# A quantised feed-forward layer spread over VectorE, GpSimd and ScalarE, and partly prepared inside the attention layer ahead of it

## The reference, cut to what matters

```
x = x + _L2_xattn_ref(_layernorm(x), ctx, ctx, mask, w_q, w_k, w_v, w_o, b_o)   # 32 heads, 8 wide
x = x + _L2_ffn_ref(_layernorm(x), w_gate, w_up, w_down)

def _act_quant(x):
    scale = 127.0 / clip(max(abs(x), axis=-1), EPS)
    return round(clip(x * scale, -128, 127)) / scale
def _bitlinear(x, w):
    return einsum('bsi,oi->bso', _act_quant(_rmsnorm(x)), _weight_quant(w))
gate = silu(_bitlinear(x, w_gate))      # 256 -> 1024
up   = _bitlinear(x, w_up)              # 256 -> 1024
return _bitlinear(gate * up, w_down)    # 1024 -> 256
```

## Time and profile before

| what | value |
|---|---|
| three runs | 1563.2, 1559.81, 1560.84 us; median 1560.84 us |
| the profiled execution | 1566.56 us, its span 1564.2 us |
| mean granted TensorE clock | 0.953 of full |
| PE busy / weight loads / DVE / ACT / POOL | 1392.5 / 878.8 / 995.0 / 728.9 / 434.4 us |
| first piece of the chain that ended last | PE 58%, DVE 23%, ACT 7%, POOL 6% |

### The profile page before, as it was taken

The page is one execution under the profiler, slowest core; times in us unless marked ns, Lnnn a source line. Parts: engine busy times, 40 slices in busy tenths (PEclk is TensorE's granted clock), DMA queues, the critical chain, the costliest instruction groups (busy, mean ns, idle before and its releaser), DMA issues.

```text
span 1564.2 us, 25737 instructions
## 1 busy us (share of the span) xinstructions
PE 1392.5 (89%) x9822; PEld 878.8 (56%) x9840; DVE 995.0 (64%) x1782; ACT 728.9 (47%) x1746; POOL 434.4 (28%) x385
## 2 busy tenths in 40 slices
PE   7869999999899789999999998988975888988889
PEld 3534555655566446665656864745652645546636
DVE  6784322225678777777776787937778676685542
ACT  3452111112777455655664456358756453362230
POOL 3230000100000387777770000100290045324100
PEclk9979999999999999999999999999997797988989
DMA  7020221003000300000001000020010100000000
GB/s 251 24 85 1 68 59 31 1 0 160 3 2 2 122 7 7 8 7 8 8 1 44 32 22 0 1 81 2 2 53 18 55 1 2 3 1 3 29 0 27
DMA packets 21852, 48.10 MB, mean 31 GB/s; under 512 B 1506, under 2 KB 16995, under 8 KB 20580
## 3 DMA queue, kind: packets, MB, share of 16 engines
q1 hardware_dynamic: 21732, 46.47, 8.5%
HBM read 41.22 MB, written 5.24 MB: 30 GB/s over the span
## 4 chain that ended last, share of the span: by engine, by line
PE 58%; DVE 23%; ACT 7%; POOL 6%; issue 5%; DMA 0%; DVEq 0%; ACTq 0%; POOLq 0%
PE PS L788 42%; DVE work L2349 5%; PE PS L1006 5%; PE PS L871 3%; PE PS L1311 2%; PE PS L800 2%; ACT work L1588 2%; DVE small L1900 2%; PE PS L1065 1%; POOL work L667 1%; POOL WB L661 1%; POOL work L664 1%; POOL WB L660 1%; PE PS L1340 1%; DVE WA L2252 1%
## 5 line engine op out<-in xcount | busy, mean ns | idle before, releaser
L788 PE MATMUL PS<-XT,WB 128*128 128x512 f32 (+1 forms) x688 | 298.3, 591 | 4.8 <-DVE XT L1926 2.4
L788 PEld LDWEIGHTS PS<-XT,WB 128*128 128x128 f32 (+1 forms) x688 | 126.1, 189 | 147.8 <-issue 143.9
L1588 ACT ACTIVATE work<-PS,small 128x128 f32<-128x128 f32 x512 | 138.0, 419 | 45.5 <-DVE small L2149 45.5
L2119 DVE TENSOR_TENSOR work<-PS,work 128x512 f32<-128x512 f32 x48 | 33.1, 692 | 168.0 <-PE PS L788 168.0
L611 POOL TENSOR_SCALAR small<-small 128x4 f32<-128x4 f32 x22 | 5.1, 231 | 413.8 <-DVE small L1903 413.7
L1544 ACT ACTIVATE work<-PS 128x512 f32<-128x512 f32 x48 | 28.7, 597 | 193.6 <-PE PS L788 193.6
L2149 DVE TENSOR_REDUCE small<-PS 128x4 f32<-128x512 f32 x128 | 80.5, 685 | 40.6 <-PE PS L788 40.5
L788 PE MATMUL PS<-XT,WA 128*128 128x512 f32 (+2 forms) x224 | 97.9, 599 | 4.8 <-DVEq L2352 2.5
L2349 DVE SCALAR_TENSOR_TENSOR work<-PS,vec,work 128x508 f32<-128x508 f32 (+2 forms) x108 | 80.2, 743 | 14.0 <-DVE work L2349 6.8
L1006 PE MATMUL PS<-WB,work 128*128 128x256 f32 x384 | 86.9, 379 | 0.5 <-DVE work L2124 0.5
L788 PE MATMUL PS<-WA,XT 128*128 128x256 f32 (+1 forms) x384 | 81.4, 374 | 3.9 <-DVE XT L2169 3.0
(11 more groups left out here) (364 smaller groups left out, 2938.9 us busy)
## 6 DMA issues: line engine op xcount, KB each, us to landing
WB<-in_l0f SPq DMA_DIRECT2D x8, 768.0 KB, 7.5
WB<-in_l1x SPq DMA_DIRECT2D x1, 6144.0 KB, 18.1
WB<-in_l0f SPq DMA_DIRECT2D x32, 96.0 KB, 6.6
WB<-in_l2f SPq DMA_DIRECT2D x1, 3072.0 KB, 10.1
WA<-in_l3a SPq DMA_DIRECT2D x1, 2624.0 KB, 9.0
WB<-in_l3f SPq DMA_DIRECT2D x1, 2064.0 KB, 7.5
WA<-in_l1f SPq DMA_DIRECT2D x1, 2056.0 KB, 10.9
C<-in_ctx SPq DMA_DIRECT2D x2, 1024.0 KB, 7.2
```

What stands on the lines that cost most here:

```text
L788: mm = lambda o, l, r, s, e: nc.tensor.matmul(o, l, r, start=s, stop=e)
L1588: f(wk(12288 + (u % 8) * G + h * P, P), bank(j)[:, h * P:(h + 1) * P], ACT.Exp, bias=sm(704 + (u % 8) * 4 + h, 1)).then_inc(*act_step(*([j ...
L2119: v.tensor_tensor(l0f_h(m)[:, lo:lo + G], bank(j), l0f_s(m)[:, lo:lo + G], ALU.mult).then_inc(*dve_step(j))
```

## The change

All of it is in l2x and l2f.

- The three sums of |w| move up to units 3, 9 and 15 and `SUMS_AT` from round 14 to 7, so POOL's nine weight passes come earlier.
- The first half of the quantised layer's input is prepared within the heads of l2x, in steps ahead of units 54, 57, 60 and 63 (`QUANT_AT`): ACT norms the four blocks, DVE takes maxima and scales, DVE scales and adds MAGIC, ACT subtracts MAGIC. It lies in `C`, which is free then. PE transposes it (`qt`) after the last `pv` of the heads.
- The second half is normed by DVE (within the first gates), rounded by POOL, and transposed by PE after the gates of block 3.
- Gates of blocks 2 apart may overlap (two gate buffers and two square buffers), and DVE frees the gate's bank.
- The passes over the hidden values leave DVE: POOL scales blocks 0 to 3 and 5 to 7 (`scale`), POOL subtracts for blocks 1, 2, 3 (`POOL_WHOLE`), ACT does both for block 4 and subtracts for 0, 5, 6, 7 (`whole`). Evacuations of the hidden transposes are shared by ACT (even blocks) and DVE (odd). PE's transposes and output products of block 0 stand ahead of and behind the last gates (`quantised_order`).
- DVE takes the maxima of blocks 0 to 3 in one go after the products of block 3.

```diff
-SUMS_AT = 14
+POOL_WHOLE = (1, 2, 3)
+QUANT_AT = (54, 57, 60, 63)
+SUMS_AT = 7
...
+def quantised_order():
+
+
+    l = [("in", b) for b in range(4)] + [("qt", 1), ("in", 4), ("in", 5), ("in", 6), ("ht", 0), ("in", 7), ("o", 0), ("ht", 1)]
+    for b in range(2, NB + 1):
+        if b < NB:
+            l += [("ht", b)]
+        l += [("o", b - 1)]
...
+            pool.wait_ge(input_scales.sem, 2)
+            for b in range(4, NB):
+                xb = XN[:, b * D:(b + 1) * D]
+                ins = nc.gpsimd.tensor_scalar(xb, xb, sm(168 + b, 1), MAGIC, ALU.mult, ALU.add)
...
+            next_step(ins)
+            nc.gpsimd.tensor_scalar(l2f_whole(1), l2f_normed(1), MAGIC, None, ALU.subtract).then_inc(whole_input.sem, whole_input.give())
+            hidden_rms(0)
+            pool.wait_ge(hidden_scales.sem, hidden_scales.next())
+            scale(0)
+            scale(1)
+            whole(1)
+            scale(2)
+            whole(2)
+            scale(3)
+            whole(3)
+            hidden_rms(1)
+            pool.wait_ge(hidden_scales.sem, hidden_scales.next())
+            for b in range(5, NB):
+                scale(b)
...
             def heads(layer):
-                for key in heads_plan():
+                for key in heads_plan(SUMS_AT if layer == "l2x" else None):
...
+                    if layer == "l2x" and key[0] == "s" and key[1] == QUANT_AT[0]:
+                        input_norm(0)
+                    if layer == "l2x" and key[0] == "s" and key[1] == QUANT_AT[3]:
+                        input_whole(0)
...
-                    if layer == "l2x" and key[0] == "s" and key[1] in (20, 26, 32):
+                    if layer == "l2x" and key[0] == "s" and key[1] in (3, 9, 15):
...
+            gates(0)
+            gates(1)
+            squares(0)
+            gates(2)
+            squares(1)
+            gates(3)
+            quantised_evac("l2f", 1)
+            squares(2)
+            squares(3)
+            gates(4)
+            gates(5)
+            squares(4)
+            whole(0)
+            gates(6)
+            hidden_evac(0)
+            gates(7)
+            squares(5)
+            squares(6)
+            squares(7)
+            hidden_evac(2)
+            h4 = wk(4 * 1024, 1024)
+            act.wait_ge(hidden_scales.sem, 2)
+            f(h4, h4, ACT.Identity, scale=sm(168 + 4, 1), bias=plus_magic).then_inc(*act_step())
+            act.wait_ge(*act_last())
+            f(wkb(14336, 8192)[:, 4 * 1024:5 * 1024], h4, ACT.Identity, bias=less_magic).then_inc(*act_step(whole_by_act))
+            whole(5)
+            hidden_evac(4)
+            whole(6)
+            whole(7)
+            hidden_evac(6)
...
+            products(0)
+            quantise_input(1, 0)
+            products(1)
+            quantise_input(1, 1)
+            products(2)
+            products(3)
+            for b in range(4):
+                maxima(b)
+            products(4)
+            hidden_factors(0)
+            products(5)
+            maxima(4)
+            products(6)
+            maxima(5)
+            products(7)
+            maxima(6)
+            maxima(7)
+            hidden_evac(1)
+            scaled_residual("l2f", 0, 200)
+            hidden_factors(1)
+            hidden_evac(3)
+            scaled_residual("l2f", 1, 200)
+            scaled_residual("l2f", 2, 200)
+            scaled_residual("l2f", 3, 200)
+            hidden_evac(5)
+            scaled_residual("l2f", 4, 200)
+            hidden_evac(7)
+            for b in range(5, NB):
+                scaled_residual("l2f", b, 200)
```

More of the change, by code:

```diff
@@ L122, in plans @@
     p["l2x"] = ln + [(k, c, g) for c in range(2) for g in range(2) for k in ("q", "k")] + [("v",), ("mask", 0), ("mask", 1)] + heads_plan(SUMS_AT)
[L123 to L129, removed]
+    l = []
+    for what, b in quantised_order():
+        if what == "in":
+            l += [(k, b, h) for h in range(2) for k in ("gate", "up")]
+        else:
+            l += [(what, b)]
     p["l2f"] = l
@@ L836, in _, with quantised_transposes @@
             pe.wait_ge(ident_in, 16)
+            def quantised_transposes(layer, g):
+                pe.wait_ge(whole_input.sem, whole_input.next())
+                o = begin(layer, "qt", g).bitcast(BF16)
+                for c in range(2):
+                    for i in range(4):
+                        ins = nc.tensor.transpose(o[:, c * G + i * P:c * G + (i + 1) * P], l2f_whole(g)[:, i * D + c * P:i * D + (c + 1) * P], identb[:, :])
+                end(ins)
             def heads(layer, wo, pad):
@@ L1782, in _, with gates @@
             heads("l2x")
[L1785 to L1796 removed]
+            def gates(b):
                 for h in range(2):
@@ new lines, in dequant, with quantise_input @@
+            def dequant(g, at, i, *to):
+                v.tensor_scalar(sm(at + 4 * g, 4), sm(160 + 4 * g, 4), 1.0 / 127.0, wm[:, i:i + 1], ALU.mult, ALU.mult).then_inc(*dve_step(*to))
+            def quantise_input(g, step):
+                normed = l2f_normed(g)
+                if step == 0:
+                    if g == 0:
+                        roots(g, input_roots)
+                    else:
+                        dve.wait_ge(pool_to_dve.sem, pool_to_dve.next())
+                        for b in range(4, NB):
+                            normalise(b)
+                if step == 1:
+                    if g == 0:
+                        dve.wait_ge(input_normed.sem, input_normed.next())
+                    v.tensor_reduce(sm(160 + 4 * g, 4), r3(normed, D), AX.X, ALU.max, apply_absolute_value=True).then_inc(*dve_step())
+                    activation_scales(g)
+                    dequant(g, 184, 0)
+                    dequant(g, 192, 1, input_scales)
+                if step == 2:
+                    for i in range(4):
+                        xb = normed[:, i * D:(i + 1) * D]
+                        v.tensor_scalar(xb, xb, sm(168 + 4 * g + i, 1), MAGIC, ALU.mult, ALU.add).then_inc(*dve_step(*([scaled_input] if i == 3 and g == 0 else [])))
+                dve.wait_ge(*dve_last())
@@ new lines, in products @@
+            def products(b):
+                for h in range(2):
+                    dve.wait_ge(act_to_dve.sem, act_to_dve.next())
+                    dve.sem_inc(bank_free[bank_of[J("l2f", "gate", b, h)]], 1)
+                    j = J("l2f", "up", b, h)
+                    dve.wait_ge(*full(j))
+                    v.scalar_tensor_tensor(wk(b * 1024 + h * G, G), bank(j), sm(192 + b, 1), l2f_gate(b)[:, h * G:(h + 1) * G],
+                                           ALU.mult, ALU.mult).then_inc(*dve_step(j))
@@ L2143, in heads @@
                     if key[0] == "s":
                         u = key[1]
+                        if layer == "l2x" and u in QUANT_AT:
+                            quantise_input(0, QUANT_AT.index(u))
                         j = J(layer, "s", u)
@@ L2493, in _ @@
-            for b in range(NB):
+            products(0)
[16 more added lines that the diff above has]
+            hidden_evac(1)
```

223 lines of the change are left out of this document (122 added, 101 removed).

## The result

| | median | lowest to highest | runs |
|---|---|---|---|
| before | 1562.02 us | 1559.81 to 1567.41 | 4 |
| changed | 1548.79 us | 1546.8 to 1550.7 | 4 |

The medians lie 13.2 us apart. The ratio is 0.9907 with an interval of [0.9882, 0.9931]; by it the change saves 14.5 us, at least 10.8. The changed kernel built once more gave 1548.59 us against 1563.68 (0.9913 [0.9894, 0.9932]). I had forecast faster, but by 7.6 us (1553.2, range from 1549.0): the sign was right, the saving I forecast was a little over half of the measured one. The profiled execution took 1549.02 us, its span 1547.2, at a mean clock of 0.956.

What follows compares the result with a forecast made beforehand. PE was taken to bound the heads, DVE three of the quantised layer's four stages. Layer 10.3 us shorter, 7.6 after the heads' 2.7: 1560.84 - 7.6 = 1553.2 us, range 1549 to 1560.5.

Steps and rivals of the forecast that it cites:

- PE's early gates: Start of the quantised layer: PE starts gates at once, with no 12 us stretch without matmuls ahead of them.
- POOL as the path between 1188 and 1203: Quantised layer: four POOL scalings and three subtractions take 12.8 us, from 1188.7 to 1201.5, while PE, DVE and ACT wait.
- The heads: Attention heads, rounds 18 to 21: the inserted preparation of the first half costs +2.7 us, bounds 0 and 8.8.
- ACT's norms: Heads: four ACT norms of 256 columns take 2.2 us, about 1.0 in ACT's idle time, 1.2 on the path.
- DVE's scalings: Heads: DVE's four scalings, in a round where DVE also adds a residual, have no slack and cost 1.1 us.
- the maxima and small steps: Heads: DVE's maxima over 1024 and six small steps, 2.4 us, add about 0.4 us.
- The sums: Heads: ACT's three sums of weight matrices, moved to rounds 1, 3 and 5, bring no change.
- the tail of the layer: End of the quantised layer: four PE transposes and five output products take 11.3 us, ending at 1217.3.
- POOL is held up by DVE: Rival, quantised layer: POOL's 17 instructions each wait 0.5 us, 5 to 8 us late, result 1558 to 1561; 14 in 100.
- The heads pay in full: Rival, heads: every insertion holds up the unit behind it, +8.8 and +2.3 for the sums, 1561.6 us; 10 in 100.
- Slower: Rival, quantised layer: POOL's scaling in place takes 3.6 us for 1024 columns, the kernel 1568 us; 8 in 100.
- More is gained: Rival: sums in idle time (-1.4), full clock over the output (-2.4) or faster POOL subtraction (-4.1): 1547 to 1550; 10 in 100.

Runs made afterwards that it cites:

- the control: The changed kernel built again with no edit, timed and profiled a second time: 1548.59 us, ratio 0.9913 to before.
- The pair with filled gaps: Idle matmuls ahead of the next layer's first transposes, nine in the kernel before, twelve in the changed one: 1559.25 us and 1548.63 us.

## Why the prediction was right in its course and wrong in its size

**What held.** PE's early gates, POOL as the path between 1188 and 1203, and who waits for whom came out as written; up to the end of ACT's passes over block 4 the sum was right: 38.8 us from the end of the heads in all four profiles of the changed kernel, 38.9 forecast (1206.0 - 1167.1; the last terms, 1.3, 0.9 and 2.1 behind 1201.5, add up to 1205.8). Rates taken from twice as wide a pass fitted: 1.11 and 2.78 us for 1.1 and 2.8. By the Trainium skill (GPSIMD Engine Reference, Elementwise side-by-side cycle accounting) the subtraction would have been an estimated 0.9 us; POOL took 2.78, so here the measurement decides. The scaling would be the same 0.9 us; it took 1.11. The heads cost 2.1 us by the means of the table (E + H 121.4 against 119.3), forecast 2.7: H alone 2.0, half for ACT's norms (forecast 1.2) and half for DVE's scalings (1.1); the maxima and small steps, put at 0.4, cost nothing. The sums cost nothing, as forecast.

**The step that failed** is the tail of the layer: "Even at full clock the evacuations of 1.0 between them hold it up, to about 10; I take 11.3". It took 8.4 us where the clock stood at half when it began, and 6.9 where it was full. Both halves of the sentence were wrong. The evacuations hold up almost nothing at full clock: PE transposes block b+1 ahead of the output product of block b, so an evacuation lies beside a product of 1.04 us, and DVE's takes 0.69 and not 1.0. In the control only the two by ACT delay a product, by a quarter us each: it starts 0.71 us behind the start of the transpose ahead of it (1209.89 to 1210.60) and not 0.45. Nor was 7.6 right for PE alone, since rows of the timeline overlap: behind a transpose of 0.61 the product starts after 0.44 (1210.68 to 1211.12). And where it begins at half clock only its first 4 us are slow (a product 1.91, a transpose 1.06); from 1210.7 in the profile above on they are 1.04 and 0.61 and the clock is full, while I had priced the leg near half clock throughout, from 1.69 and 1.0. Against a mean of 7.7 us the term was 3.6 us too long. Behind it 0.7 went back, as the next layer's first transpose came 2.6 to 2.7 us behind the last product, where the forecast had 1.9 (1.1 for the last residual, and the 0.8 from the end of the stage at 1228.7 to that transpose in before). The layer is 13.9 us shorter by the means of the table (49.1 against 63.0) and not 10.3; that profile of before which I worked from, with 62.4, explains 0.6 of it.

**The rest of the miss** is outside the changed stretches, where I had put nothing. The mean spans differ by 16.0 us (1564.7 and 1548.7): layer -13.9, heads +2.1, R -2.7 and everything ahead of the heads -1.5, the latter two in code that is the same in both kernels. The timed runs give 13.2 and 15.1 us by their medians, 14.5 and 13.6 by their ratios. The 11.8 us of heads and layer are shown; the 1 to 3 us beyond them lie in unchanged parts. There the clock differs with the time: from 9 us behind the start of R to the end it is 0.89, 0.89 and 0.92 in the three profiles of before (326, 326 and 317 us) and 0.90 in all four of the changed kernel (320 to 321). So R differs by 9.5 us within before, and its mean by 2.7 between the kernels. The pair with filled gaps differs by 10.6 us (1559.25 - 1548.63), which agrees with 11.8 and with the thought that before loses a little more clock at the seam; that this is a property of the kernels and not of the executions that were profiled stays open. What decides whether the tail begins at half or full clock was not settled either. It goes with the heads: in the six profiles in which the layer is that of the changed kernel, the tail took 6.9 us in the three where E is 93.1 or 93.2, and 8.4 in the three where it is 92.2 to 92.6. No run shows why.

**The rivals.** "POOL is held up by DVE" fell: beside DVE's products and maxima its scalings and subtractions ran at 1.1 and 2.8 us. It is true in another place, which the changed kernel avoids: beside DVE's passes from f32 into bf16 a root went from 1.04 to 2.22 us. The Trainium skill (SBUF - State Buffer, two separate sides) has a DVE instruction in a two-port mode shut GpSimd out while it runs. The trace agrees if these passes run in such a mode, which no run here shows; they took 0.64 us each for 1024 columns, where a maximum took 1.21. "The heads pay in full" fell by 2.1 against 8.8. "Slower" fell with the scaling at 1.11 us instead of 3.6. "More is gained" is what happened, in part for one of the three reasons it gave, the clock over the output (full in two profiles of four), and for those that it didn't have, the cheap evacuations and the overlap of PE's rows. With 10 in 100 it had too little, and the lower edge of my range, 1549.0, lay in the middle of its 1547 to 1550.

## What to carry to other kernels

Work under another layer's critical engine is nearly free if it is cut into pieces and each lies in an idle gap of its engine; here 11 us between the heads and the first gate became 2 us within the heads. Look then for what these pieces wait for on a third engine: a root of 1 us at the end of a queue of long passes cost 29 us. In pricing a tail, follow the program's order to see which evacuations lie beside matmuls, price PE at both clocks and let it recover within the tail, and let the range hold both.

## What was not expected of the hardware

- Executions of before differ by 12 us within one series (1555.4 to 1567.4, and 1557.3 to 1569.3), and one single run took 1572.4, in stretches whose instructions are the same. At one place it is visible: 48 matmuls took 11.3 us at a clock of 0.58 and 7.4 at 1.00. An edit worth 2 us needs its stretch read from the traces.
- Twelve needless products in a gap of 2.65 us did not fix what came behind it: the transposes took 3.0 us, where without them they took 2.9 or 3.55, and the products after them 5.04 or 3.76. In the kernel before, nine such products made the whole faster by 3.6 us.
- A scaling with a per-partition factor took POOL 1.11 us for 1024 columns, a subtraction of a constant into bf16 2.78, two and a half times as much.
